# Two graph layers in one kernel: dense chunks last and downwards, the last two tiles as groups of their own, two ring halves joined on VectorE

## The reference

```
h  = relu(layernorm(x))
x1 = x + concat(h @ W_self.T, (segment_sum(e64 @ W_edge.T, dst) / degree) @ W_neigh.T) @ W_final.T + b_final
h2 = relu(layernorm(x1))
x2 = x1 + relu(concat(h2, segment_sum(e128, dst)) @ W1 + b1) @ W2 + b2
```

## Time and profile before

| | |
|---|---|
| runs, median (lowest to highest) | 534.71 us (531.97 to 535.15) |
| the profiled execution: its time | 538.03 us |
| its span, first to last instruction | 536.2 us |
| mean granted clock of TensorE | 0.978 of full speed |
| TensorE busy (products) | 494.8 us, 92% |
| VectorE busy | 416.8 us, 78% |
| GpSimd busy | 382.9 us, 71% |
| ScalarE busy | 178.5 us, 33% |
| DMA | 169.55 MB, mean 316 GB/s |

### The profile page before, as it was taken

One profiled execution on the slowest core, in us unless ns is written; L12 is line 12 of the kernel. 1 busy time (PEld: TensorE's weight loads), 2 busy tenths in 40 slices (PEclk: granted clock), 3 DMA queues, 4 the chain that ended last, 5 costly groups with the idle time before them and its releaser, 6 DMA issues.

```text
span 536.2 us, 26042 instructions
## 1 busy us (share of the span) xinstructions
PE 494.8 (92%) x10913; PEld 440.6 (82%) x10913; DVE 416.8 (78%) x1403; ACT 178.5 (33%) x397; POOL 382.9 (71%) x523
## 2 busy tenths in 40 slices
PE   8999788899989989989999999999999899999995
PEld 7889788798867878878887888789787788888784
DVE  5848989779994769978899679989969789956422
ACT  0011024243524234542525242534433362312201
POOL 2799586878696764897778977697975585863820
PEclk9997999999997989999999999999999899999998
DMA  8998999999995999999999999999999899987801
GB/s 280 398 363 293 377 372 353 364 325 363 334 329 188 343 345 299 361 312 321 368 343 381 300 343 328 377 322 316 366 339 326 278 337 325 315 306 264 335 23 33
DMA packets 113231, 169.55 MB, mean 316 GB/s; under 512 B 5486, under 2 KB 84310, under 8 KB 113111
## 3 DMA queue, kind: packets, MB, share of 16 engines
q1 hardware_dynamic: 85843, 154.42, 82.3%
q10 hardware_dynamic: 27268, 13.43, 8.7%
HBM read 161.43 MB, written 6.40 MB: 313 GB/s over the span
## 4 chain that ended last, share of the span: by engine, by line
PE 75%; DVE 10%; issue 9%; POOL 4%; DVEq 1%; ACT 0%; ACTq 0%; POOLq 0%
PE ps L644 25%; PE ps L662 14%; PE ps L646 5%; PE ps L731 5%; PE ps L710 5%; PE ps L722 4%; PE ps L691 4%; PE ps L682 4%; PE ps L724 3%; DVE agg L1080 2%; DVE onehot L1050 2%; POOL hot_sum L530 2%; POOL hot_part L530 1%; PE ps L583 1%; PE ps L596 1%
## 5 line engine op out<-in xcount | busy, mean ns | idle before, releaser
L644 PEld LDWEIGHTS ps<-onehot,ring 128*64 128x64 f32 x3126 | 194.6, 139 | 32.0 <-issue 25.6
L644 PE MATMUL ps<-onehot,ring 128*64 128x64 f32 x3126 | 213.3, 225 | 6.9 <-issue 6.3
L646 PE MATMUL ps<-onehot,ring 128*64 128x64 f32 x3126 | 213.8, 225 | 6.3 <-issue 6.1
L646 PEld LDWEIGHTS ps<-onehot,ring 128*64 128x64 f32 x3126 | 194.8, 139 | 7.6 <-issue 7.6
L530 POOL TENSOR_TENSOR hot_part<-onehot 128x384 bf16<-128x384 f32 (+2 forms) x128 | 118.0, 922 | 113.9 <-DVE onehot L1050 110.9
L1050 DVE TENSOR_TENSOR onehot<-iota_win,rel 128x384 f32<-128x384 f32 (+3 forms) x192 | 168.8, 880 | 0.2
L1080 DVE TENSOR_TENSOR agg<-ps,agg 128x128 f32 (+1 forms) x319 | 94.8, 297 | 85.2 <-PE ps L671 61.0
L662 PE MATMUL ps<-onehot,ring 128*64 128x64 f32 x3126 | 120.4, 224 | 7.6 <-issue 7.4
L662 PEld LDWEIGHTS ps<-onehot,ring 128*64 128x64 f32 x3126 | 107.9, 140 | 7.7 <-issue 7.4
L530 POOL TENSOR_TENSOR hot_sum<-hot_part 128x128 bf16<-128x128 bf16 x96 | 52.9, 551 | 7.5
L897 ACT ACTIVATE hn<-x,nmr,rstd 128x128 f32<-128x128 f32 x98 | 40.3, 483 | 19.9 <-DVE nmr L1142 19.9
(11 more groups left out here) (127 smaller groups left out, 648.5 us busy)
## 6 DMA issues: line engine op xcount, KB each, us to landing
ring<-in_edge_attr_dram SPq DMA_DIRECT2D x95, 768.0 KB, 5.5
ring<-in_edge_attr_dram SPq DMA_DIRECT2D x96, 384.0 KB, 7.1
ring<-in_edge_attr_dram SPq DMA_DIRECT2D x32, 832.0 KB, 5.9
ring<-in_edge_attr_dram SPq DMA_DIRECT2D x32, 416.0 KB, 7.6
x<-in_x_dram ACTq DMA_DIRECT2D x23, 256.0 KB, 7.1
out_dram<-x ACTq DMA_DIRECT2D x23, 256.0 KB
x<-in_dst_dram SPq DMA_DIRECT2D x1, 384.0 KB
x<-in_dst_dram SPq DMA_DIRECT2D x1, 208.0 KB, 3.5
```

Source lines behind the costliest of these rows:

```text
L644: nc.tensor.matmul(bank[0:H, o:o + WIN], ring128[0:K, slot, u, 0:H], hots, start=u == 0, stop=r == R - 1, skip_group_check=True)
L646: nc.tensor.matmul(bank[H:P, o:o + WIN], ring128[0:K, slot, u, H:D], hots, start=u == 0, stop=r == R - 1, skip_group_check=True)
```

## The change

The dense chunks are taken downwards, 14 to 0. Nodes 128 to 255 become a group of their own (number 25, called SECOND, q = 24), complete at tick 121, and nodes 0 to 127 stay as group 0 (q = 25, the last, tick 128); each has one tile. Both use two products per tile in `neigh` and are not merged. For q = 22 and 23 VectorE adds the columns of the upper ring to those of the lower ring in all three planes (`join`), one tick before TAKE; the groups are then merged as all others are, and `neigh` and `hidden` read one place. SyncE waits for and loads the flag before it waits for the stores. By the planner, TAKE, NEIGH and SELF of q = 0 to 23 stay as they were; q = 24 has NEIGH 121 and SELF 111, q = 25 has NEIGH 128 and SELF 118. The rest of the diff adapts indices.

```diff
-    ORDER += range(DENSE)
+    ORDER += reversed(range(DENSE))
...
-    NG = 1 + -(-(N - FIRST_W) // GW)
+    SECOND = 1 + -(-(N - FIRST_W) // GW)
+    NG = SECOND + 1
     def begin_of(g):
-        return FIRST_W + (g - 1) * GW if g else 0
+        return P if g == SECOND else FIRST_W + (g - 1) * GW if g else 0
...
-    MERGED = [q for q, g in enumerate(SEQ[:-1]) if g not in BOTH]
-    NEIGH = [t + 2 if q < NG - 1 else t for q, t in enumerate(TAKE)]
+    MERGED = [q for q, g in enumerate(SEQ) if 0 < g < SECOND]
+    JOINED = [q for q, g in enumerate(SEQ) if g in BOTH]
+    NEIGH = [t + 2 if 0 < g < SECOND else t for g, t in zip(SEQ, TAKE)]
...
# SyncE
             for t in range(1, CH):
                 load_edges(t)
+            sp.wait_ge(s_gen, 1)
+            again = sp.value_load(gen[0:1, 0:1], min_val=0, max_val=1)
             sp.wait_ge(s_store, 16 * (NG + 1))
...
-            otherwise(sp, general)
+            with sp.If(again > 0):
+                general()
...
# TensorE, neigh
-                parts = [(a, k) for a in columns_of(g) for k in range(1 if q in MERGED else 2)]
+                parts = [(columns_of(g)[0], k) for k in range(1 if q in MERGED else 2)]
...
# TensorE, hidden
-                for i, a in enumerate(columns_of(g)):
-                    nc.tensor.matmul(ps_hid[:, 0:w], w1b[:], agg[:, 0, a:a + w], start=i == 0, stop=False)
+                a = columns_of(g)[0]
+                nc.tensor.matmul(ps_hid[:, 0:w], w1b[:], agg[:, 0, a:a + w], start=True, stop=False)
...
# ScalarE, swap
+                if q in JOINED:
+                    act.wait_ge(s_join, JOINED.index(q) + 1)
...
# VectorE
+            def join(q):
+                lower, upper = columns_of(SEQ[q])
+                dve.wait_ge(s_added, ADDED[min(CH, TAKE[q])])
+                nc.vector.tensor_tensor(agg[:, :, lower:lower + GW], agg[:, :, upper:upper + GW], agg[:, :, lower:lower + GW],
+                                        ALU.add).then_inc(s_join, 1)
...
                     for i, (q, _) in enumerate(FOLDS):
                         if t == TAKE[q] - 1:
                             fold(i)
+                    for q in JOINED:
+                        if t == TAKE[q] - 1:
+                            join(q)
```

More of the change, by code:

```diff
@@ L99, in build_gnn @@
     SPLIT = low
-    ORDER += range(DENSE)
+    ORDER += reversed(range(DENSE))
     SIDE += ["dense"] * DENSE
     AT = {c: t for t, c in enumerate(ORDER)}
-    NG = 1 + -(-(N - FIRST_W) // GW)
+    SECOND = 1 + -(-(N - FIRST_W) // GW)
+    NG = SECOND + 1
     def begin_of(g):
-        return FIRST_W + (g - 1) * GW if g else 0
+        return P if g == SECOND else FIRST_W + (g - 1) * GW if g else 0
     def end_of(g):
-        return min(N, begin_of(g + 1))
+        return P if g == 0 else FIRST_W if g == SECOND else N if g == SECOND - 1 else begin_of(g + 1)
     def tiles_of(g):
@@ L126, in build_gnn @@
         lo, hi = place(first_edge(c), -1), place(first_edge(c + 1) if c < CH - 1 else E, 1) + WIN
-        reach.append([0] if side == "dense" else [g for g in range(NG) if lo < end_of(g) and hi >= begin_of(g)])
+        reach.append([g for g in (0, SECOND) if lo < end_of(g) and hi >= begin_of(g)] if side == "dense" else [g for g in range(NG) if lo < end_of(g) and hi >= begin_of(g)])
     READY = [max(t for t in range(CH) if g in reach[t]) + 1 for g in range(NG)]
@@ L138, in build_gnn @@
     BOTH = [g for g in LOWER if g in UPPER]
-    MERGED = [q for q, g in enumerate(SEQ[:-1]) if g not in BOTH]
-    NEIGH = [t + 2 if q < NG - 1 else t for q, t in enumerate(TAKE)]
-    FOLDS = [(q, a) for q, g in enumerate(SEQ) if g % 4 == 1
+    MERGED = [q for q, g in enumerate(SEQ) if 0 < g < SECOND]
+    JOINED = [q for q, g in enumerate(SEQ) if g in BOTH]
+    NEIGH = [t + 2 if 0 < g < SECOND else t for g, t in zip(SEQ, TAKE)]
+    FOLDS = [(q, a) for q, g in enumerate(SEQ) if g % 4 == 1 and g < SECOND
              for a in ([FIRST_W] if g > 1 and g in LOWER else []) + ([UPPER_AT] if g in UPPER else [])]
     def columns_of(g):
-        at = [(0 if g == 0 else FIRST_W + (g - 1) % 4 * GW)] if g in LOWER else []
+        at = [(begin_of(g) if g in (0, SECOND) else FIRST_W + (g - 1) % 4 * GW)] if g in LOWER else []
         return at + ([UPPER_AT + (g - 1) % 4 * GW] if g in UPPER else [])
@@ L154, in build_gnn @@
     for q, g in enumerate(SEQ):
-        for at, other in ((FIRST_W, g + 4 if g and g in LOWER else 0), (UPPER_AT, g - 4 if g in UPPER else 0)):
-            if other in (LOWER if at == FIRST_W else UPPER) and other:
+        for at, other in ((FIRST_W, g + 4 if 0 < g < SECOND and g in LOWER else 0), (UPPER_AT, g - 4 if g in UPPER else 0)):
+            if other in (LOWER if at == FIRST_W else UPPER) and 0 < other < SECOND:
                 a = at + (g - 1) % 4 * GW
@@ L167, in bounds @@
         if SIDE[t] == "dense":
-            return 0, FIRST_W
+            return 0, FIRST_W if TAKE[TURN[SECOND]] > t else P
         done = CLEARS[:cleared(t)]
-        free = {g for g in range(NG) if TAKE[TURN[g]] > t}
+        free = {g for g in range(SECOND) if TAKE[TURN[g]] > t}
         if SIDE[t] == "bottom":
@@ L182, in bounds @@
         lo = hi
-        while lo - 1 in UPPER and lo - 1 in free and (lo - 1 > NG - 5 or NEIGH[TURN[lo + 3]] + 11 <= t):
+        while lo - 1 in UPPER and lo - 1 in free and (lo - 1 > SECOND - 5 or NEIGH[TURN[lo + 3]] + 11 <= t):
             lo -= 1
-        return begin_of(lo), N + WIN if hi == NG - 1 else begin_of(hi + 1)
+        return begin_of(lo), N + WIN if hi == SECOND - 1 else begin_of(hi + 1)
     for t in range(CH):
@@ L212, in x_done @@
     def x_done(q):
-        return sum(32 if SEQ[k] == NG - 1 else 16 for k in range(q % X_SEMS, q + 1, X_SEMS))
+        return sum(32 if SEQ[k] == SECOND - 1 else 16 for k in range(q % X_SEMS, q + 1, X_SEMS))
     HOT_SUMS, ADDED, LOADED, in_slot = [0], [0], [], [0] * SLOTS
@@ L356, in build_gnn @@
         s_tp, s_tpc, s_row, s_rowc, s_self = (sem(n) for n in ("s_tp", "s_tpc", "s_row", "s_rowc", "s_self"))
-        s_swap, s_merged, s_fold, s_nb, s_deg, s_x1, s_bn2, s_mv2, s_std2, s_rstd2, s_nmr2 = (
-            sem(n) for n in ("s_swap", "s_merged", "s_fold", "s_nb", "s_deg", "s_x1", "s_bn2", "s_mv2", "s_std2", "s_rstd2", "s_nmr2"))
+        s_join, s_swap, s_merged, s_fold, s_nb, s_deg, s_x1, s_bn2, s_mv2, s_std2, s_rstd2, s_nmr2 = (
+            sem(n) for n in ("s_join", "s_swap", "s_merged", "s_fold", "s_nb", "s_deg", "s_x1", "s_bn2", "s_mv2", "s_std2", "s_rstd2", "s_nmr2"))
         s_h2, s_x1b, s_hid, s_hr, s_store = (sem(n) for n in ("s_h2", "s_x1b", "s_hid", "s_hr", "s_store"))
```

11 lines of the change are left out of this document (6 added, 5 removed).

## The result

The changed kernel takes 532.92 us, median of 20 runs (528.11 to 537.2), against 535.13 us, median of 20 runs of the kernel before. The ratio is 0.9944 with a 95% interval of 0.9918 to 0.9970: 3.0 us less. The forecast was 8.45 us less. The time lies outside of the range that was given, 1.4 us above its upper end. A second comparison gave 0.9930 (0.9891 to 0.9968), 3.7 us less.

The account below looks back on a forecast made before the run. TensorE, with nearly no idle time, was taken to bound the kernel: 7.0 us off it before the last chunk ends, 0.65 for the tail and 0.8 for the flag make 8.45, so 534.71 becomes 526.3 us; range 522.3 to 531.5.

Parts of the forecast that it names:

- the third reading of what bounds the kernel: The chain of waits runs along TensorE's own instructions, so time off it before tick 127 comes off the end.
- Neighbour and hidden products: TensorE, q = 22 and 23: merged groups need fewer neighbour products, 5.7 us off, and one ring's hidden sums, 1.7 us off.
- Joins and merges: VectorE, ticks 112 to 115: 2.2 us a join, no TensorE wait (bounds 0 and 3 us); GpSimd collision 0 to 1.3.
- Extra group: Group 25 before the last chunk: two more neighbour products on TensorE, +0.45 us; its load and store cost nothing.
- Tail: Behind the last chunk: one tile less, but q = 24's steps cross; -0.65 us, bounds no gain and -1.9.
- Flag: At the end, SyncE's flag load moved ahead of the store wait saves 0.8 us; bounds 0.5 and 0.8.
- B: VectorE late at the second merge, 3 us wait plus 1.7 us of low clock: 531.0 us; chance 0.13.
- D: One more TensorE stall that no engine ended, with its clock, 4.4 us back: 530.7 us; chance 0.07 with F.
- F: Loads bind: ticks 118 to 127 needed 7 us sooner, against 10.5 us of cover; 1 in 100, in D's place.
- C: Joins at ticks 112 and 114 run at the fold's price, 11.1 us each; slower, 543.9 us; chance 0.06.
- E: Tail and flag give nothing, leaving 7.0 us of gain: 527.7 us; chance 0.14.

Follow-up runs that it names:

- a_up: The changed kernel with the dense chunks upwards in two runs, 7 to 14, then 0 to 6; ratio 0.9853 against the kernel before.
- a_pad64busy: The changed kernel with 16 unused products in tick 60 and the tail's twelve unused products moved behind q = 24's output; 0.9875 against the kernel before.
- a_nojoin: The changed kernel without the joins, keeping order, extra group and early flag; 1.0068 against the kernel before, 3.6 us slower.
- b_join: The kernel before with the joins and the two merges alone; 5.5 us less than before, 6.4 in the repeat.
- b_joinflag: The kernel before with joins, merges and early flag, without new order and extra group; 6.5 us less than before, 6.1 in the repeat.
- After2: The changed kernel, unchanged, profiled a second time; stage from tick 113 to 127 60.30 us, against 61.87 in the first profile.
- a_light: The changed kernel with loads from tick 113 on fetching 16 columns instead of a chunk; stage 57.09 us, against 61.36 for the kernel before with such loads.
- a_pad128: The changed kernel with 32 unused products (128 entries) in tick 60; 0.4 us slower than the kernel before, stage 61.1 us.
- b_reverse: The kernel before with the dense chunks downwards and nothing else; 0.36% slower, 0.34% in the repeat.

## Why the prediction was wrong

**The step that failed** is the third reading of what bounds the kernel: "time taken off TensorE before tick 127 comes off the end, as long as nothing else becomes late". Something else was late already: the next block of TensorE's own program, for which the sum had no term. The stages with little idle time in the earlier trace rows hid that this program arrives at a pace little above its need; the trace of before has two stalls of this kind in the same stage, 1.1 and 1.0 us, and one of 2.67 us in the earlier trace rows. I had read the latter as chance that the change doesn't touch. The waits of TensorE from 400 us on, which I had seen before predicting, list all five such stalls, the two of the stage among them; I hadn't asked what they have in common. In the changed kernel such stalls rose from 2.09 to 5.87 us. That the products were priced rightly is shown by the sum, which holds within 1 us in 17 profiles. That the stalls are the program's is shown by their entries, and that the loads delay it by their absence without loads.

**Neighbour and hidden products.** Right: 32 instructions became 8 in 0.89 us; L717 has 200 instructions where L710 had 248. The joins alone take 6.6 us off the stage (mean of four profiles, 57.54 against 64.15), of 7.46.

**Joins and merges.** Right in size, and TensorE didn't wait for them; but 2.2 us was in part luck, as GpSimd's work in the same ticks shows:

```profile
459.89 1.00 POOL L537 TENSOR_TENSOR hot_part<-onehot 128x384 bf16<-128x384 f32 x1 [0.56 <-DVE onehot L1059]
...
460.97 1.83 POOL L537 TENSOR_TENSOR hot_sum<-hot_part 128x128 bf16<-128x128 bf16 x1
462.88 0.43 POOL L537 TENSOR_TENSOR hot_sum<-hot_sum,hot_part 128x128 bf16<-128x128 bf16 x1
...
468.60 1.13 POOL L537 TENSOR_TENSOR hot_part<-onehot 128x384 bf16<-128x384 f32 x1
```

The first join began at 460.12, when `hot_part` still had 0.77 us to go, and took 2.39; the second at 469.21, when it had 0.52 us to go, and took 2.13. Take these times off and 1.62 and 1.61 us are left, and so it is for all 24 joins in the 12 profiles that have them (1.61 to 1.62). So each join stood until GpSimd's instruction had ended, and then GpSimd stood: its `hot_sum`, started at 460.97, ended at 462.80, 0.3 us behind the join's end at 462.51, and took 1.83 us where the next one took 0.43. The Trainium skill, page "SBUF — State Buffer", section "Who interferes with whom", would have one of the two engines stand for the other's whole instruction; these rows agree. Of the 0 to 1.3 us kept for this the joins paid 0.8 and 0.5, beside the 1.6 us that they need. The merges of the earlier trace rows hold such waits too (the longest, 1.28 us, stood 0.73), so that three times their median came out near the joins' 2.1 to 2.4 us though a wait doesn't grow with the columns.

**Extra group.** Priced at 0.45 us for its products, and that fits the sum. Together with the new order it has a cost in the profiles that I didn't see: seven profiles with joins, extra group and new order have stages of 58.6 to 62.2 us (mean 60.4), four with joins alone 57.0 to 58.3 (mean 57.5). 0.45 of these 2.9 us are products; stalls and falls are the rest. The runs say so of the changed kernel, by less: -3.0 and -3.7 us, with a shorter tail, against -5.5 to -6.5. They don't say so of a_up (-7.9) and a_pad64busy (-6.7), which have joins, extra group and a new order too. By themselves the parts don't settle it: a_nojoin has 1.6 us of stalls, and the order alone 4.5 in one profile and 2.1 in the other. Why the changed kernel stalls more than the joins alone, with blocks of the same size and loads of the same size, stays open.

**Tail.** Right in size. The addition of the last group's result:

```profile
522.02 0.39 PE L738 MATMUL ps<-w,hid 128*128 128x128 f32 x2
...
522.45 0.29 DVE L1218 TENSOR_TENSOR x<-ps,x 128x128 f32<-128x128 f32 x1 [1.35 <-PE ps L738]
...
522.84 0.21 DVE L1210 TENSOR_SCALAR nmr<-mv,rstd 128x1 f32<-128x1 f32 x1
523.23 0.49 ACT L946 ACTIVATE h<-x,nmr,rstd 128x128 f32<-128x128 f32 x1 [1.79 <-DVE nmr L1210]
...
525.93 0.29 DVE L1218 TENSOR_TENSOR x<-ps,x 128x128 f32<-128x128 f32 x1 [2.87 <-PE ps L738]
```

From the last chunk's end (518.09) to the end of the last addition 8.13 us, against 9.02 before: -0.9 for -0.65. The factors (L1210) end at 523.05, 4.96 us behind the chunk, for the 5.3 of the prediction; and they stand behind the result of q = 24, as it had said: that addition waits for TensorE's output, which waits behind unused products.

**Flag.** SyncE's branch came at 529.73, when the last store was told, and the span ended at 530.4: 0.7 us later, against 1.2 before, 0.5 us saved. The tails of b_join and b_joinflag say 0.7 on the mean; 0.8 was taken, with 0.5 as the lower bound.

**The rivals.** The measured 532.92 lies above B (531.0) and D (530.7), which were nearest by their number. Of the two, D, one stall more with its clock, has the kind of loss, though not its reason: it had counted on chance. After2 is its picture in detail, a 2.35 us stall and a fall. It had 0.07 with F. B's mechanism is real and shows in a_light, 1.8 us; in the kernel as it is the stalls cover it. C is refuted by joins of 2.1 to 2.4 us. E is refuted by the tail. F is refuted: the loads themselves landed at least 6.2 us before their use in the stage, in each profile; they did their harm to another transfer.

Whether paced loads would take the stalls away wasn't tried. The best kernels of the study, joins with the flag (0.9878 and 0.9886), the changed kernel with shifted blocks and unused products (0.9875), and a_up (0.9853), can't be told apart.

## What to carry to other kernels

When TensorE is the bound and the profile puts its few idle times down to nobody, list them by place: if they fall on the same instructions in each run, a fixed count apart, the program itself comes late, and part of the time that a change removes may come back as such stalls. Price a removal with and without that, and look whether full-rate loads lie beside it; test it by making these loads tiny for some ticks. And time a kernel with a few unused instructions put far ahead, and take off the time that they need themselves: if it still moves by as much as your change, you measure the place of the program's pieces too.

## What the runs showed of the hardware

- TensorE's program arrives in transfers of 16 KB, one for 256 of its rows in the trace (a float32 product is four, two instructions with a weight load each, and waits count too). A transfer takes about 1 us. At the 47 stalls of the stages its block was in use 1.1 to 1.6 us after its end, and it had started 2.7 to 5.5 us (once 7.9) behind the entry into the block before; with the loads gone it was mostly 0.1 to 0.9 us.
- The stalls from it are up to 3.6 us long. Five (2.67 us at 420.26 before, 2.35 in after2, 2.39 in a_up, 3.58 in a_pad128, 1.92 in a_pad64busy) were followed by about 4 us at 0.5 to 0.6 of the clock; b_reverse's, of 3.41 us, was not.
- An addition of 128 x 1,536 float32 with both inputs in the same memory took 2.1 to 2.4 us on VectorE in 24 joins. Of this 0.5 and 0.8 us were waits for the GpSimd instruction under way when it began; what is left is 1.61 to 1.62 us each time. The GpSimd instruction behind it ended 0.3 us after it.
